# Expert products of the second batch in split form, weights split during the search, and another scatter order

## The reference, cut to what matters

```
x = layernorm(X + differential_attention(X))        # 8 heads of width 128, two softmaxes a head
scores = softmax(x @ gate_w)                        # 8 experts
top_p, top_idx = top_k(scores over tokens, 256)     # for each batch and expert: 256 of 1024 tokens
xin = x[top_idx]                                    # (2, 8, 256, 128)
h = gelu(xin @ w1)                                  # "up": 128 -> 512
y = (h @ w2) * top_p                                # "down": 512 -> 128
out = zeros; out[top_idx] += y
x = layernorm(x + out)
```

## Time and profile before

| | us |
|---|---|
| median of 3 runs | 915.63 |
| lowest, highest | 915.50, 916.42 |
| the profiled execution | 908.3 |
| its span (first to last instruction in the trace) | 906.4 |
| PE busy | 865.1 (95%) |
| ACT busy | 724.9 (80%) |
| DVE busy | 664.0 (73%) |
| POOL busy | 625.3 (69%) |

### The profile page before, as it was taken

How to read it: one execution, slowest core, us unless ns; L and a number is a source line. 1 busy time by engine, 2 the same in 40 slices (tenths; PEclk the granted TensorE clock), 3 DMA queues, 4 the chain that set the end, 5 groups by cost and what they waited for, 6 DMA issues and landing times.

```text
span 906.4 us, 14690 instructions
## 1 busy us (share of the span) xinstructions
PE 865.1 (95%) x4574; PEld 725.9 (80%) x4576; DVE 664.0 (73%) x1113; ACT 724.9 (80%) x1389; POOL 625.3 (69%) x1012
## 2 busy tenths in 40 slices
PE   6889999999999999999999999999999999988991
PEld 5668888888888888888888888888888888777991
DVE  5777777778777777777777777778898787367153
ACT  4888888888888888898889888888888889554523
POOL 1777767767776777676778867667766677845772
PEclk9999999999999999999999999999999999999996
DMA  6010110202020201001000020000000001622243
GB/s 184 9 54 29 45 39 4 79 1 82 0 82 1 71 13 59 12 19 53 1 30 1 19 58 18 15 18 16 17 14 1 19 1 35 199 70 21 50 77 78
DMA packets 44845, 36.16 MB, mean 40 GB/s; under 512 B 6192, under 2 KB 42576, under 8 KB 44512
## 3 DMA queue, kind: packets, MB, share of 16 engines
q1 hardware_dynamic: 40864, 31.69, 11.6%
q0 software_dynamic: 3904, 3.54, 2.5%
HBM read 24.86 MB, written 14.55 MB: 43 GB/s over the span
## 4 chain that ended last, share of the span: by engine, by line
PE 80%; POOL 7%; issue 4%; DVE 3%; ACT 3%; DMA 2%; another core or an unknown queue 1%; SPq 0%; POOLq 0%; DVEq 0%; ACTq 0%
PE t_ps L1533 11%; PE ring_a L1494 6%; PE ring_a L1496 6%; PE ring_a L1495 6%; PE ring_b L1494 6%; PE u_ps L1494 6%; PE ring_b L1496 6%; PE u_ps L1496 6%; PE ring_b L1495 6%; PE u_ps L1495 6%; PE o_ps L1494 2%; PE o_ps L1495 2%; PE o_ps L1496 2%; PE x_ps L1494 2%; PE x_ps L1496 1%
## 5 line engine op out<-in xcount | busy, mean ns | idle before, releaser
L656 POOL TENSOR_TENSOR attn<-prob 128x1024 f32<-128x1024 f32 x128 | 307.6, 2403 | 172.5 <-ACT prob L797 158.7
L1033 DVE TENSOR_TENSOR at_lo<-t_ps,at_hi 128x512 fp32r<-128x512 f32 x253 | 174.1, 688 | 99.4 <-ACT at_hi L780 99.2
L1026 DVE TENSOR_REDUCE negmax<-ring_a 128x1 f32<-128x1024 f32 x128 | 156.7, 1224 | 58.5 <-PE ring_a L1496 55.7
L780 ACT ACTIVATE at_hi<-t_ps 128x512 fp32r<-128x512 f32 x253 | 151.6, 599 | 38.9 <-PE t_ps L1533 37.7
L1026 DVE TENSOR_REDUCE negmax<-ring_b 128x1 f32<-128x1024 f32 x128 | 156.1, 1220 | 1.9 <-PE ring_b L1496 0.3
L1533 PE MATMUL t_ps<-ident,attn 128*128 128x128 f32 x1012 | 152.1, 272 | 4.3 <-DVE at_lo L1033 4.1
L797 ACT ACTIVATE prob<-prob,coef 128x1024 f32<-128x1024 f32 x128 | 147.6, 1153 | 5.7 <-POOL coef L620 5.6
L1533 PEld LDWEIGHTS t_ps<-ident,attn 128*128 128x128 f32 x1012 | 124.5, 140 | 30.0 <-DVE at_lo L1033 9.4
L791 ACT ACTIVATE prob<-ring_a,negmax 128x1024 f32<-128x1024 f32 x128 | 143.1, 1118 | 4.6 <-DVE negmax L1026 4.1
L791 ACT ACTIVATE prob<-ring_b,negmax 128x1024 f32<-128x1024 f32 x128 | 142.4, 1113 | 0.6 <-DVE negmax L1026 0.5
L1494 PE MATMUL ring_b<-xt_hi,q_hi 128*128 128x512 f32 x256 | 111.5, 436 | 0.0
(11 more groups left out here) (429 smaller groups left out, 1625.3 us busy)
## 6 DMA issues: line engine op xcount, KB each, us to landing
w_copy<-in_L_ffn_w SPq DMA_DIRECT2D x16, 256.0 KB, 3.5
q_hi<-w_copy SPq DMA_DIRECT2D x8, 256.0 KB, 5.5
q_lo<-w_copy SPq DMA_DIRECT2D x8, 256.0 KB, 6.1
ww_dram<-ww_hi SPq DMA_DIRECT2D x8, 192.0 KB, 2.5
ww_dram<-ww_lo SPq DMA_DIRECT2D x8, 192.0 KB, 2.8
ww_hi<-ww_dram SPq DMA_DIRECT2D x8, 192.0 KB, 2.4
ww_lo<-ww_dram SPq DMA_DIRECT2D x8, 192.0 KB, 2.5
wq_s<-in_L_attn_Wq SPq DMA_DIRECT2D x8, 128.0 KB, 3.3
```

Of the source, the lines that this page charges most:

```text
L656: pool.tensor_tensor(attn[:, t % AB, :], prob[:, t % 2, 1, :], prob[:, t % 2, 0, :], ALU.add).then_inc(attn_ready, 1)
L780: act.activation(at_hi[:, g % 2, half * GT:(half + 1) * GT, c], t_bank(t, half)[:, :].rearrange("p (k q) -> p k q", q=P), ACT.Copy).then_i ...
L1026: dve.tensor_reduce(negmax[:, par, m:m + 1], ring[m][:, :], axis=AX.X, op=ALU.max, negate=True).then_inc(negmax_ready, 1)
L1033: dve.tensor_tensor(at_lo[:, g % 2, k, c], t_bank(t, half)[:, :].rearrange("p (k q) -> p k q", q=P), at_hi[:, g % 2, k, c].bitcast(F32), A ...
```

## The change

It has five parts.

1. The up products of jobs 8 to 15 become three fp32r products each. `w1_hi` and `w1_lo` hold the split first weights of the eight experts in tiles that the attention has left (`at_hi`, `at_lo`); `xs_hi` and `xs_lo` hold the split rows.
2. The weights are split during the search: after each of `ffn(1)` to `ffn(8)` ACT rounds one expert's weights (`w_round`, 128x512), and POOL subtracts (`w_lower`, 128x512).
3. The rows of jobs 8 to 15 are rounded by ACT where they were copied, and DVE makes their lower part (`xs_lower`, 128x256); PE's `up` waits for it.
4. `scatter(3)` moves ahead of batch 1's gathers, and ACT's `y_scale(7)` ahead of its two sign instructions. After the gathers the order of scatters is 4, 5, 8, 6, 7, 9 (before: 3, 4, 5, 6, 7, 8, 9). Jobs 8 and 9 have a semaphore of their own, `scattered_x`.
5. In the last layernorm ACT makes the squares of the first four tiles of batch 1, in place of DVE's `late_squares(0)`.

The diff without its declarations of semaphores:

```diff
@@ -192,6 +192,9 @@
         raws = [w_home(e) for e in range(E)]
+        w1_hi, w1_lo = ([t[:, 0].rearrange("p k n -> p (k n)")[:, e * F:(e + 1) * F].rearrange("p (f c) -> p f c", f=FT)
+                         for e in range(E)] for t in (at_hi, at_lo))
+        xs_hi, xs_lo = ([xk_part(t, 0)[:, n * CAP:(n + 1) * CAP] for n in range(2)] for t in (xk_hi, xk_lo))
         xs = [t[:, :, :].rearrange("p m d -> p (m d)") for t in (wq_s, wk_s)]
@@ -498,8 +503,7 @@
                         x2_in[h], 16)
-            for n in range(2):
-                sp.wait_ge(scattered[n], 16 * CT * (E + SC) // 2)
+            sp.wait_ge(scattered_x, 16 * CT * SC)
             sp.wait_ge(xg_stored[1], 16)
@@ -681,17 +685,22 @@
                     pool.wait_ge(acc_stored, 32)
-                    need(pool, scattered[(q - 1) % 2], 16 * CT * ((q + 1) // 2))
+                    need(pool, scattered_x, 16 * CT * (q - E))
                     for k in range(CT):
...
                                                 in_offset=None, bounds_check=N - 1,
-                                                compute_op=ALU.add).then_inc(scattered[q % 2], 16)
+                                                compute_op=ALU.add).then_inc(scattered_x, 16)
                     return
...
                                             compute_op=ALU.add).then_inc(scattered[q % 2], 16)
+
+            def w_lower(e):
+
+                pool.wait_ge(w_hi_done, e + 1)
+                pool.tensor_tensor(w1_lo[e], raws[e][:, 0], w1_hi[e].bitcast(F32), ALU.subtract).then_inc(w_split, 1)
 
@@ -733,13 +742,15 @@
             pool.iota(tok_row, pattern=[[1, N]], base=0, channel_multiplier=0).then_inc(row_ready, 1)
-            for q in range(3):
-                scatter(q)
+            for e in range(E):
+                w_lower(e)
+                if e in (2, 4, 6, 7):
+                    scatter((2, 4, 6, 7).index(e))
             gather_ready(1)
...
                     gather_rows(q, k)
-            for q in range(3, E + SC):
+            for q in (4, 5, E, 6, 7, E + 1):
                 scatter(q)
@@ -835,11 +846,18 @@
 
+            def w_round(e):
+
+                if e == 0:
+                    act.wait_ge(u_ready, 31)
+                act.wait_ge(w_in[e % WSEM], w_count(e))
+                act.activation(w1_hi[e], raws[e][:, 0], ACT.Copy).then_inc(w_hi_done, 1)
+
             def xs_round(q):
...
                 need(act, up_ready, 2 * (q - 1))
-                act.activation(xs[q % 2], xs_ps[q % 2], ACT.Copy).then_inc(xs_copied, 1)
+                act.activation((xs if q < E else xs_hi)[q % 2], xs_ps[q % 2], ACT.Copy).then_inc(xs_copied, 1)
 
@@ -853,7 +871,7 @@
                 q, half = n // 2, n % 2
-                if 0 <= n - 3 < CT * (E + SC):
+                if 0 <= n - 3 < CT * (E + SC) and n != LAST[LEVELS - 1] + 1:
                     y_scale(n - 3)
@@ -943,6 +961,9 @@
                 ffn(n)
+                if 0 <= n - 1 < E:
+                    w_round(n - 1)
+            y_scale(LAST[LEVELS - 1] - 2)
             signs(1, 0)
@@ -953,6 +974,8 @@
                 ln_squares(2, c)
+            for c in range(GT):
+                ln_squares(3, c)
             act.wait_ge(ln_fac, 4)
@@ -1093,7 +1116,8 @@
                 else:
-                    dve.wait_ge(late_sq, QT)
+                    dve.wait_ge(ln_sq, 2 * QT + GT)
+                    dve.wait_ge(late_sq, GT)
                 dve.tensor_scalar(stat[:, 1, c], stat[:, 0, c], 1.0 / D, EPS, ALU.mult, ALU.add).then_inc(ln_var, 1)
@@ -1310,9 +1334,19 @@
 
+            def xs_lower(q):
+
+                dve.wait_ge(xs_copied, q + 1)
+                dve.tensor_tensor(xs_lo[q % 2], xs_ps[q % 2], xs_hi[q % 2].bitcast(F32),
+                                  ALU.subtract).then_inc(xs_split, 1)
+
             def ffn(n):
...
                 q, half = n // 2, n % 2
+                if n == 2 * E:
+                    xs_lower(E)
+                if half == 0 and E < q + 1 < JOBS:
+                    xs_lower(q + 1)
                 m = n - 3
@@ -1478,7 +1512,6 @@
                 ln_means(3, h)
-            late_squares(0)
             ln_vars_end(0)
@@ -1780,7 +1813,10 @@
                     pe.wait_ge(y_added, TILES - 3 * (1 - q))
-                need(pe, xs_copied, q - 1)
+                if q - 2 < E:
+                    need(pe, xs_copied, q - 1)
+                else:
+                    pe.wait_ge(xs_split, q - 1 - E)
                 for k in range(CT):
@@ -1789,11 +1825,18 @@
                 if half == 0:
-                    pe.wait_ge(xs_copied, q + 1)
-                    if q < E:
+                    if q >= E:
+                        pe.wait_ge(xs_split, q + 1 - E)
+                        pe.wait_ge(w_split, E)
+                    else:
+                        pe.wait_ge(xs_copied, q + 1)
                         pe.wait_ge(w_in[q % WSEM], w_count(q))
...
                 for f in range(2 * half, 2 * half + 2):
+                    if q >= E:
+                        last_u = three(up_ps[half][:, (f % 2) * CAP:(f % 2 + 1) * CAP], w1_hi[q % E][:, f, :],
+                                       w1_lo[q % E][:, f, :], xs_hi[q % 2], xs_lo[q % 2])
+                        continue
                     last_u = pe.matmul(up_ps[half][:, (f % 2) * CAP:(f % 2 + 1) * CAP], raws[q % E][:, 0, f, :],
```

More of the change, by code:

```diff
@@ L325, in build @@
             sem("xs_ready"), sem("xs_copied"), sem("up_ready"), sem("gelu_ready"))
+        w_hi_done, w_split, xs_split = sem("w_hi_done"), sem("w_split"), sem("xs_split")
+        scattered_x = sem("scattered_x")
         y_ready, y_scaled, y_split = sem("y_ready"), sem("y_scaled"), sem("y_split")
```

## The result

| | median | runs | ratio to before |
|---|---|---|---|
| before, in this comparison | 915.63 us | 915.39 to 916.51 | |
| changed kernel | 919.59 us | 918.06 to 921.47 | 1.0031 [1.0017, 1.0045] |
| forecast | 907.6 us | 904.8 to 912.5 | |

The changed kernel is 0.3% slower; the profiled execution took 919.59, its span is 917.8. One plain fact is needed to read this number: kernels here are timed under one of two conditions, which change between occasions, even on one chip. Under condition A the kernel before takes 908, under condition B 916. The comparison above was made under B; the profile from which I predicted (908.3) is a run under A. I did not know this, and it is most of the story. The traces tell the two apart: under B some updates of PE's semaphores come several us behind the products they tell of, under A none does.

The account below looks back on a forecast made before the run. POOL's queue was taken to set the end through job 9's last scatter; 7.15 from it plus 0.9 from the layernorm made 8.05, so 900.25 profiled and, with the 7.33 offset, 907.6 us, range 904.8 to 912.5.

Parts of the forecast that it names:

- the rate rival: PE's up products: fp32r products of 256 columns cost 0.22 instead of 0.12, giving 915.5 us; chance 0.09.
- forecast 2.3: PE's up products of batch 1: three fp32r products save 0.14 in each of 16 halves, 2.3 us.
- 8.05: Whole kernel: total saving, 7.15 from POOL's last scatter plus 0.9 from the last layernorm.
- 7.15: POOL's queue, main term: job 9's last scatter lands at 883.65 instead of 890.79, 7.15 us earlier.
- 3.24 later: End of POOL's queue: job 9's last scatter lands 3.24 us after its start.
- the layernorm's 0.9: Last layernorm: four squares on ACT let the first power start 0.2 after the last mean, saving 0.9 us.
- same offset: Timed median over profiled execution: the 7.33 us difference stays, turning 900.25 profiled into 907.6.
- PE has some 7 us of room: End of the kernel before: POOL's queue sets the end, and PE has some 7 us of room.
- 1.0 ahead of the load: End of PE's work: transposes of the sum are through by 886.7, 1.0 us ahead of the load at 887.7.
- the sum had 0.5: PE's start on batch 1: job 9's later gather moves the up products from 843.96 to 844.45, 0.5 us lost.
- the blocked rival: Search: DVE's counts and POOL's subtractions block each other, up to 10.4 us over the search, 918.0 us; chance 0.06.

Follow-up runs that it names:

- a1_after: The changed kernel, unaltered, profiled again on the first follow-up occasion (kernel before 908.29): 901.06 us, ratio 0.9917.
- a0_before: The kernel before, unaltered, run again on the first follow-up occasion (before 908.29): ratio 1.000.
- a0_before_4: The kernel before, unaltered, traced on the fourth occasion, where before takes 915.26: 914.93 us.
- a1_after_2: The changed kernel, unaltered, once more on the second occasion, where before takes 915.82: 917.1 us, ratio 1.0006.
- e3: The changed kernel with `w_lower(7)` moved behind job 9's gathers, on the fifth occasion (before 908.28): 904.63 us, ratio 0.9948.
- e1: The changed kernel with `w_lower(7)` moved behind job 9's gathers, on the second occasion (before 915.82): 911.25 us, ratio 0.9945.
- h1: The changed kernel with batch 1's sixteen gathers replaced by SP's plain loads of fixed rows, third occasion (before 908.46): 902.54 us, ratio 0.9934.
- h2: The changed kernel with batch 1's gathers as SP's plain loads of fixed rows, fourth occasion (before 915.26): 902.08 us, ratio 0.985.
- e2: The changed kernel with `w_lower(7)` moved behind job 9's gathers, a second time under condition B: 909.1 us, ratio 0.9938.
- interleaved form: The changed kernel with scatters 4 and 5 mixed in among batch 1's gathers: 900.87 us, ratio 0.991; again 903.38, ratio 0.9938.

## Why the prediction was wrong, step by step

*What held*, by `a1_after` (condition A). POOL before the gathers: `w_lower` 1.28 (taken 1.30); scatter 0 not moved; first gather 837.12 (837.65). The counts of the search are untouched even under B:

```profile
809.40 1.28 DVE L1242 TENSOR_SCALAR_CACHE_REDUCE attn<-prob,cand 128x1024 f32<-128x1024 f32 x1
...
811.80 1.28 DVE L1242 TENSOR_SCALAR_CACHE_REDUCE attn<-prob,cand 128x1024 f32<-128x1024 f32 x1
```

POOL behind them: last scatter at 880.38, forecast 880.4, no wait. The other accumulator: loaded at 880.63 and added from 883.52 to 885.5 (880.1; 883 to 885). The products of 256 columns (lines of the changed kernel's first profile; the median of 80 distances in `a1_after` is 0.12 too):

```profile
872.36 0.28 PE L1529 MATMUL ring_a<-xk_hi,at_lo 128*128 128x256 f32 x1
872.47 0.28 PE L1527 MATMUL ring_a<-xk_hi,at_hi 128*128 128x256 f32 x1
```

They are 0.12 apart at the full clock; the rate rival is dead. From the first of batch 1's products to the last transposes PE takes 887.04 - 846.25 = 40.79, against 885.89 - 842.70 = 43.19 in `a0_before`: 2.4 saved (forecast 2.3). Layernorm: the first power 0.33 behind the last mean (889.36), 0.9 less than the 1.24 before. Span 899.0 for 898.35.

*What is luck in this.* The search of `a1_after` began 1.2 earlier than in the trace that I predicted from (first count at 806.46 for 807.65). Beside `a0_before` (806.38) the span is 6.3 shorter, not 8.05, and by the medians of the two occasions under A 7.2 and 6.5 were saved. Two terms of the sum were too good. The last scatter starts 6.2 earlier (880.38 for 886.59), not 7.15. And the "3.24 later" of its landing became 4.2: SP can load `acc_x1` only at 884.56, having issued the load of the other accumulator at 880.63, right behind the last scatter. That took back the layernorm's 0.9. Two small misreadings had no effect: from 857.16 to 874.65 ten scatters start, not nine (the distance of 1.94 is right), and the count of the earlier trace rows isn't wholly beside POOL's addition but begins 0.09 ahead of it.

*What failed.* First, "the median of the runs shown, 915.63, is 7.33 above the profiled one; with the same offset". That offset is no constant of the kernel. It is what is left of PE's loss under condition B when the room on PE is taken off, and the text had named that room itself: "PE has some 7 us of room", and "1.0 ahead of the load" afterwards.

| | condition | first count of the search | last transposes | between | span |
|---|---|---|---|---|---|
| before, `a0_before` | A | 806.38 | 885.89 | 79.51 | 905.3 |
| before, `a0_before_4` | B | 806.17 | 900.30 | 94.13 | 912.7 |
| changed, `a1_after` | A | 806.46 | 887.04 | 80.58 | 899.0 |
| changed, first profile | B | 807.00 | 905.95 | 98.95 | 917.8 |
| changed, `a1_after_2` | B | 808.41 | 903.92 | 95.51 | 915.7 |
| `w_lower(7)` late, `e3` | A | 810.33 | 890.05 | 79.72 | 902.8 |
| `w_lower(7)` late, `e1` | B | 806.57 | 895.74 | 89.17 | 907.6 |
| plain loads, `h1` | A | 808.72 | 889.10 | 80.38 | 900.8 |
| plain loads, `h2` | B | 810.41 | 891.09 | 80.68 | 902.8 |

In the kernel before the last transposes are 14.4 later under B and the span 7.4 longer: it hides 7.0. In the changed kernel they are 18.9 and 16.9 later and the span 18.8 and 16.7 longer: it hides nothing. The change moved the end from POOL's queue to where POOL and PE end together, and under B, PE alone counts. There POOL's 7.15 is off the path.

Second, a smaller step: PE was to reach the transposes of job 8's rows at 842.4, start batch 1's products at 844.45 and reach the sum at 884.5. It transposed at 844.90 and started at 846.25. Against `a0_before` (842.70) that is 3.5 later, where the sum had 0.5, and so PE ended 1.15 later instead of 1.8 earlier. DVE's comparison of 128x256 stood 2.65 instead of 0.35 beside POOL's subtraction, and PE waited for what DVE makes next:

```profile
833.28 0.20 PE L1655 MATMUL x_ps<-tok_rows,pick 128*128 128x8 bf16 x2 [2.73 <-DVE pick L1313]
...
834.71 3.10 PE L1853 MATMUL ring_b<-q_lo,attn 128*128 128x128 f32 x16
```

That wait was 0.42 in `a0_before`, and what follows it starts 2.4 later (833.28 for 830.89). Behind it the granted clock is 0.5 from 833.7 to 837.1, which costs 1.3, of which `y_scale(7)` ahead of the signs gives 0.6 back. The last 0.45 is `xs_lower`, which the gather for job 8 does not cover (0.75 of wait for 0.30). This is the blocked rival, at a place where I had not looked: I priced it on the counts, which are immune, and not on the plain comparison that follows them. Under A it costs POOL 0.83, since POOL waits 1.13 for the indices, of which 0.30 is issue. It costs PE most of its room.
The Trainium skill (SBUF — State Buffer, Who interferes with whom) says that a DVE operation in its two-port mode or with two SBUF inputs needs the ports that it shares with GpSimd alone. The runs are in line with it for this comparison and POOL's two-input subtraction (2.65 beside it, 0.35 without), if the comparison, which has one tensor input, runs in the two-port mode; no row names its mode. For POOL's descriptor writing they show no such wait: 0.35 beside a scatter's issue.

Why ratio 1.003 and 1.0006 rather than an equal end? From the first count to the last transposes the kernel before takes 14.6 more under B than under A, the changed one 18.4 and 14.9. It is 1.1 longer already under A, and behind the last transposes its layernorm gives 0.6 back under B (11.8 to the end of the span for 12.4). The rest is what PE loses beyond the 14.6, 0.3 to 3.8, and the start of the search. With one trace of before under B and two of the changed kernel it isn't shown that the change loses more; its products do have one more hand-over per job (`xs_copied`, then `xs_split`), each of which can be late. With the same hand-overs `e1` and `e2` lose only 9.5 and 9.2 against `e3`. With plain loads 0.3 is lost.

## What to carry to other kernels

When the timed runs stand above the profiled one, find out what the difference is made of before adding it to a forecast: a cost that is partly hidden grows when a change uses up what hides it. Room on the second engine is part of what a kernel is worth, and a change that makes two engines end together gives it away. A two-input POOL operation over SBUF is best placed where DVE's plain operations aren't on the path; the accumulating counts didn't mind it.

The fastest real kernel under B was `e1`/`e2` (0.994), under A the changed kernel and its interleaved form (0.991 to 0.994). Over both, `w_lower(7)` behind job 9's gathers is the version to keep: 0.9945, 0.9938 and 0.9948.

## What the runs showed of the hardware

- Under a condition that comes and goes on one chip, PE's semaphore updates come up to 8.9 us (changed kernel, first profile), 9.5 (`a0_before_4`) and 9.7 (`e1`) behind the modelled end of the matmul while POOL issues 16 indirect gathers of 128 rows, one every 1.31 us. PE loses 14.6 to 18.4 us over them and the scatters behind them (9.5 and 9.2 in `e1` and `e2`). With as many rows by plain loads it loses 0.3. What the condition is, and what in the gathers does it, is open.
- POOL's indirect DMAs themselves keep their pace under it: 21.1 from the first gather to the first scatter (837.67 to 858.81), as in the earlier trace rows.
- An idle PE came back at the granted clock of 0.5: eight products of 128 columns in 2.04 to 2.08 instead of 1.05. Under A it did so behind a wait of 2.73.
- A stretch of 3.4 us at the granted clock of 0.5 ahead of the search moved its start by 1 to 2 us; from none to two of them occur, in both kernels and under both conditions.
